# Inverse roots of the second layer's head norms: from GpSimd's power to Newton steps on VectorE

## The reference, cut to what matters

```python
attn = jax.nn.softmax(A1, -1) - lam * jax.nn.softmax(A2, -1)
O = jnp.einsum('bhqk,bhkd->bhqd', attn, V)
rms = jnp.sqrt(jnp.mean(O * O, -1, keepdims=True) + EPS)      # EPS = 1e-05
O = O / rms * rms_scale * (1.0 - LAMBDA_INIT)                 # LAMBDA_INIT = 0.8
O = O.transpose(0, 2, 1, 3).reshape(B, N, H * 2 * dh)
return O @ W_o.T
```

## Time and profile before

| what | us |
|---|---|
| timed runs | 1345.17, 1341.36, 1341.60 |
| median | 1341.6 |
| profiled execution, first to last instruction (span) | 1322.9 |
| PE busy in the span | 974.1 (74%) |
| DVE busy | 844.9 (64%) |
| ACT busy | 582.7 (44%) |
| POOL busy | 437.1 (33%) |
| mean granted TensorE clock | 0.852 of full |

### The profile page before, as it was taken

The page is one execution under the profiler, slowest core; times in us unless marked ns, Lnnn a source line. Parts: engine busy times, 40 slices in busy tenths (PEclk is TensorE's granted clock), DMA queues, the critical chain, the costliest instruction groups (busy, mean ns, idle before and its releaser), DMA issues.

```text
span 1322.9 us, 17363 instructions
## 1 busy us (share of the span) xinstructions
PE 974.1 (74%) x5741; PEld 575.7 (44%) x5741; DVE 844.9 (64%) x1977; ACT 582.7 (44%) x1409; POOL 437.1 (33%) x624
## 2 busy tenths in 40 slices
PE   6361565984985996888788878887878787776693
PEld 3241232453453564333334534444455454455583
DVE  1588879769988432665676656566555677644764
ACT  4344252462442343254454444344455554455363
POOL 0201441723724123022443132426311328433242
PEclk9685686996987998797898898778799999899897
DMA  7300000001000001000000000003134304233183
GB/s 223 110 0 0 1 0 1 1 1 36 1 1 1 0 1 42 7 1 0 1 1 1 1 0 0 1 0 117 56 109 128 106 16 131 67 119 104 54 270 114
DMA packets 54313, 60.40 MB, mean 46 GB/s; under 512 B 6208, under 2 KB 40656, under 8 KB 54224
## 3 DMA queue, kind: packets, MB, share of 16 engines
q1 hardware_dynamic: 52176, 55.10, 13.5%
q0 software_dynamic: 2048, 4.20, 1.0%
HBM read 46.05 MB, written 13.24 MB: 45 GB/s over the span
## 4 chain that ended last, share of the span: by engine, by line
PE 49%; DVE 22%; ACT 11%; issue 9%; POOL 6%; DMA 1%; SPq 0%; DVEq 0%; POOLq 0%; ACTq 0%
PE banks L792 8%; PE banks L849 5%; PE banks L935 5%; PE banks L839 4%; DVE MX L1444 3%; PE banks L627 3%; PE banks L802 3%; POOL oms L1943 3%; PE banks L805 2%; PE banks L679 2%; PE banks L867 2%; PE banks L909 2%; ACT PT L1760 2%; ACT yh L1695 2%; PE banks L874 2%
## 5 line engine op out<-in xcount | busy, mean ns | idle before, releaser
L1444 DVE TENSOR_REDUCE MX<-banks 128x4 f32<-128x512 f32 (+2 forms) x192 | 199.4, 1043 | 95.4 <-PE banks L909 93.6
L1920 POOL TENSOR_SCALAR_AFFINE_SELECT PT<-PT 128x256 f32<-128x256 f32 x256 | 105.9, 427 | 410.3 <-ACT PT L1760 410.1
L1760 ACT ACTIVATE PT<-banks 128x768 f32<-128x768 f32 (+1 forms) x192 | 168.0, 878 | 108.9 <-PE banks L867 108.1
L792 PE MATMUL banks<-xgT,wg 128*128 128x128 f32 x616 | 85.3, 282 | 39.2 <-ACT ysb L1721 35.7
L935 PE MATMUL banks<-PT,VA 128*17 128x512 f32 (+3 forms) x1024 | 101.5, 496 | 16.8 <-DVE on L1467 16.6
L874 PE MATMUL banks<-KS,QS 32*128 32x512 f32 (+3 forms) x512 | 97.8, 426 | 19.7 <-DVE MX L1444 15.2
L839 PE MATMUL banks<-w,hid 128*128 128x128 f32 x512 | 78.2, 301 | 45.5 <-DVE hid L1389 43.2
L839 PEld LDWEIGHTS banks<-w,hid 128*128 128x128 f32 x512 | 70.8, 209 | 79.9 <-DVE hid L1389 61.1
L867 PE MATMUL banks<-QS,KS 32*128 32x128 f32 (+3 forms) x512 | 94.0, 412 | 14.1 <-ACT PT L1760 9.0
L792 PEld LDWEIGHTS banks<-xgT,wg 128*128 128x128 f32 x616 | 74.4, 191 | 52.8 <-issue 50.4
L867 PEld LDWEIGHTS banks<-QS,KS 32*128 32x128 f32 x512 | 45.0, 196 | 95.4 <-issue 52.3
(11 more groups left out here) (273 smaller groups left out, 2055.2 us busy)
## 6 DMA issues: line engine op xcount, KB each, us to landing
wg<-in_ffn_dram SPq DMA_DIRECT2D x77, 386.0 KB, 3.3
yb<-ysb SPq DMA_DIRECT2D x17, 256.0 KB, 3.7
xg<-xs SPq DMA_DIRECT2D x16, 256.0 KB, 3.1
w<-in_ffn_w_dram SPq DMA_DIRECT2D x12, 256.0 KB, 5.2
xs<-zt SPq DMA_DIRECT2D x2, 1472.0 KB, 14.4
xs<-zt SPq DMA_DIRECT2D x1, 1984.0 KB, 13.3
x<-in_L_attn_x_dram SPq DMA_DIRECT2D x4, 256.0 KB, 5.0
out_dram<-x SPq DMA_DIRECT2D x16, 64.0 KB
```

What stands on the lines that cost most here:

```text
L792: mm = e.matmul(ps[:, at:at + cols], w, h, start=True, stop=True)
L1444: v_mx.at(e.tensor_reduce(MX[n % 2][:, u:u + nm, qb % 2, 2 * pair:2 * pair + 2, 24].rearrange("p s i -> p i s"), p4, AX.X, ALU.max, negate ...
L1760: a_p.at(e.activation(PT[q % 3][:, 2 * pair:2 * pair + 2, :], where["score", q, pair][:, :, 0:n], ACT.Exp, scale=ISQ8))
L1920: ins = e.affine_select(out=pt, in_=pt, compare_op=ALU.is_ge, fill=0.0, base=0, pattern=[[0, 2], [1, 128]], channel_multiplier=-1)
```

## The change

Step 3 goes away. DVE's `rms` takes over the inverse root itself: it halves the mean (times 1/32 plus 0.5e-5), makes a first guess of the root by integer-like arithmetic on the bits of the float (times -0.5 plus a constant, read and written as int32), and does three Newton steps of three instructions each, y <- y * (y*y*o - 1.5). Each instruction waits for the one before it. The three sign changes leave a negative root, for which the learned scale `rsc` gets the opposite sign. The roots are in a new tile `root`. `rms_o` waits for DVE's own semaphore. In the table `rms_o` moves from t + 6.5 to t + 4.0.

```diff
-        table += [(t, ("rms", n, part)), (t + 3.5, ("rms_p", n, part)), (t + 6.5, ("rms_o", n, part))]
+        table += [(t, ("rms", n, part)), (t + 4.0, ("rms_o", n, part))]
...
-        pw64 = sb("pw64", [128, 64])
...
+        root, step_ = sb("root", [128, 64]), sb("step", [128, 64])
...
-                v_own.at(e.tensor_scalar(rsc[:, :], rs0[:, :], 1.0 - 0.8, None, ALU.mult))
+                v_own.at(e.tensor_scalar(rsc[:, :], rs0[:, :], 0.8 - 1.0, None, ALU.mult))
...
             def rms(b, part):
-                o = means[:, :, heads[part]]
+                o, y, t = (tile[:, :, heads[part]] for tile in (means, roots, steps))
                 v.wait_ge(g_sq, 3 * b + part + 1)
                 n = v_own.at(e.tensor_reduce(o, osq[:, :, heads[part], :], AX.X, ALU.add))
                 v.wait_ge(v_own, n)
-                v_ms.at(e.tensor_scalar(o, o, 1.0 / 16.0, 1e-5, ALU.mult, ALU.add))
+                n = v_own.at(e.tensor_scalar(o, o, 1.0 / 32.0, 0.5e-5, ALU.mult, ALU.add))
+                v.wait_ge(v_own, n)
+                n = v_own.at(e.tensor_scalar(y.bitcast(mybir.dt.int32), o.bitcast(mybir.dt.int32), -0.5, 1593268703.0,
+                                             ALU.mult, ALU.add))
+                for i in range(3):
+                    v.wait_ge(v_own, n)
+                    n = v_own.at(e.tensor_tensor(t, y, y, ALU.mult))
+                    v.wait_ge(v_own, n)
+                    n = v_own.at(e.tensor_tensor(t, t, o, ALU.mult))
+                    v.wait_ge(v_own, n)
+                    n = v_own.at(e.scalar_tensor_tensor(out=y, in0=t, scalar=-1.5, in1=y, op0=ALU.add, op1=ALU.mult))
+                pr["root", b, part] = n
 
             def rms_o(b, part):
-                v.wait_ge(g_rs, 3 * b + part + 1)
+                v.wait_ge(v_own, pr["root", b, part])
...
-            def rms_p(b, part):
-                h0, h1 = PARTS[part]
-                o = oms[:, :].rearrange("p (q h) -> p q h", q=4)[:, :, h0:h1]
-                g_.wait_ge(v_ms, 3 * b + part + 1)
-                g_rs.at(e.tensor_tensor(o, o, pw64[:, 0:4 * (h1 - h0)].rearrange("p (q h) -> p q h", q=4), ALU.pow))
-
...
-            e.memset(pw64[:, :], -0.5)
```

More of the change, by code:

```diff
@@ L492, in build @@
             signal(n) for n in ("p_s", "a_p", "g_sel", "p_pv", "a_ov", "p_ot1", "v_on", "g_om"))
-        g_sq, v_ms, g_rs, v_o, p_to, a_to, p_wo1, v_xq, g_x1 = (
-            signal(n) for n in ("g_sq", "v_ms", "g_rs", "v_o", "p_to", "a_to", "p_wo1", "v_xq", "g_x1"))
+        g_sq, v_o, p_to, a_to, p_wo1, v_xq, g_x1 = (
+            signal(n) for n in ("g_sq", "v_o", "p_to", "a_to", "p_wo1", "v_xq", "g_x1"))
         p_tb, a_tb, v_out, v_xm, v_po, v_oh = (Signal(old.sem, 4) for old in (p_wo, a_oT, v_xt, v_dk, v_gm, v_vb))
@@ L1472, in _ @@
             width = [h1 - h0 for h0, h1 in PARTS]
-            means = oms[:, :].rearrange("p (q h) -> p q h", q=4)
+            means, roots, steps = (tile[:, :].rearrange("p (q h) -> p q h", q=4) for tile in (oms, root, step_))
             def rms(b, part):
-                o = means[:, :, heads[part]]
+                o, y, t = (tile[:, :, heads[part]] for tile in (means, roots, steps))
                 v.wait_ge(g_sq, 3 * b + part + 1)
@@ L1479, in rms @@
                 v.wait_ge(v_own, n)
-                v_ms.at(e.tensor_scalar(o, o, 1.0 / 16.0, 1e-5, ALU.mult, ALU.add))
+                n = v_own.at(e.tensor_scalar(o, o, 1.0 / 32.0, 0.5e-5, ALU.mult, ALU.add))
[10 more added lines that the diff above has]
+                pr["root", b, part] = n
             def rms_o(b, part):
-                v.wait_ge(g_rs, 3 * b + part + 1)
+                v.wait_ge(v_own, pr["root", b, part])
                 sq = osq[:, :, heads[part], :]
-                n = v_own.at(e.tensor_tensor(sq, om[b % 2][:, :, heads[part], :], means[:, :, heads[part]].unsqueeze(3)
+                n = v_own.at(e.tensor_tensor(sq, om[b % 2][:, :, heads[part], :], roots[:, :, heads[part]].unsqueeze(3)
                                              .broadcast_to([128, 4, width[part], 16]), ALU.mult))
@@ L1960, in _ @@
                         o_pw=o_pw, o_dk=o_dk, o_ol=o_ol, down=down, spread=spread, collect=collect,
-                        moe_x=moe_x, score=score, o_norm=o_norm, rms=rms,
-                        rms_p=rms_p, w_o=w_o)
+                        moe_x=moe_x, score=score, o_norm=o_norm, rms=rms, w_o=w_o)
             for job in order(table0, LATE0["POOL"]):
```

## The result

| | us (median, lowest to highest) | to before [95%] |
|---|---|---|
| before, measured beside it | 1343.38 (1341.36 to 1348.49) | |
| changed | 1362.38 (1358.03 to 1365.08) | 1.0136 [1.0102, 1.0171] |

The changed kernel is 19 us slower; +6.0 was forecast and the range ended at 1353. The sign was right, the size was three times too small. The profiled execution took 1358.03 us for a span of 1356.3 at a mean granted clock of 0.839.

The account below looks back on a forecast made before the run. The prediction saw no full engine but a web of short waits. Site gains and losses summed to +6.5 us, collisions and unseen slack to -0.5, so 1341.6 + 6.0 = 1347.6 us, with a range of 1335 to 1353.

Parts of the forecast that it names:

- the site walk: At each of the twelve normalization sites, PE's work shifted by the changed waits; gains and losses sum to +6.5 us.
- 1.0: Site with 32 columns: `rms_o` makes the second top 2.8 us later; a loss of 1.2 us was taken.
- 2.0: Site with 32 columns: 2.3 us of idle won against a 2.2 us block, second top late; loss 0.6 us.
- The stretch from 640 to 860 us: Six sites, 0.0 to 1.2, forecast to grow by +5.1 us together; no growth would prove the prediction wrong.
- Collisions with selects: Newton instructions on DVE beside POOL's selects: up to 0.2 us more each, adding 0 to 4 us in all.
- POOL's relief: The 45 us of powers taken off POOL; claimed to count nothing by itself.
- 17.1 us of idle against 25.2 of work: On DVE: idle before line 1485 that the power causes, traded for the Newton block's work at twelve sites.
- The chain's 33 us: Power's share of the chain from 600 us on, at eight of twelve sites; the prediction told readers to mistrust it.
- Rival (a): Chain view right: 33 us less 17 us of block, so -16, 1325.6 us; chance 0.16 in full or part.
- (b): Only DVE's balance counts and the new order is free: +3.4, 1345.0 us; chance 0.29 together with (c).
- (c): The web of waits absorbs both signs: 1341.6 us, plus or minus 2; chance 0.29 together with (b).
- (d): Newton meets selects at most sites, block 2.7 us instead of 2.1: 5.4 us added, 1353.0 us; chance 0.09.

Follow-up runs that it names:

- e4: Changed kernel without its three Newton steps, the root only guessed from the bits: 1315.49 us, 0.9775 of before.
- e8: Changed kernel with the three Newton steps at three places in DVE's list and `rms_o` back at t + 6.5: 1335.13 us, 0.9928 of before.
- e13: Changed kernel with sixteen spare PE matmuls before each of four waits for `v_o`: 1346.78 us, 1.0126 of before.
- e5: Changed kernel with POOL's twelve powers put back on a tile that nobody reads: 1353.86 us, 1.0072 of before.
- e15: The same kernel as e5, run again on another chip: 1338.64 us, 1.0076 of before.
- e12: Kernel before, power kept, with ten DVE instructions behind each `rms` whose results nobody reads: 1358.32 us, 1.0149 of before.
- e10: Changed kernel with two Newton steps, one in `rms` and one before `rms_o` at t + 6.5: 1331.73 us, 0.9915 of before.
- e3: Kernel before with POOL's power kept and only `rms_o` moved to its new place, t + 4.0: 1356.43 us, 1.0074 of before.
- e9: Changed kernel, no further edit, timed and profiled again: 1362.89 us, 1.0174 of before.

## Why the prediction was right in sign and wrong in size

**The step that failed** is the sum of the site walk, +6.5 us. It moved every PE instruction by the delay of what it waits for, and gave it the duration it had in the trace of before. That holds for the waits: of the 15.4, 20.3 and 13.0 us by which the stretch grew against the second profile of before, 6.3, 5.1 and 2.7 are waits. The other 9.1, 15.2 and 10.3 are matmuls that take longer, and the granted clock is lower there (0.87, 0.86 and 0.86 against 0.88). The walk had put this term at nothing. The prediction had the means for it: the earlier trace rows show a granted clock of 0.67 at 1.0, and it used 1.12 against 0.66 us for the four transposes there, to place an end, but never asked what the new waits would do to the clock. e4, e8 and e13 carry this: fewer waits, or none at one place, and the same matmuls are shorter at once. That a long wait lowers the clock is shown by filling one (e13 at 0.2). That the new waits at 2.0, 2.2 and 3.0 did is read from the order of events; no run fills those.

**Site by site.** Line 867's and the later matmuls' shifts give, from the first profile of before to the changed one, about -3.6 at 0.0, +1.0 at 0.1, +1.9 at 0.2, +2.6 at 1.0, +3.4 at 1.1, +2.5 at 1.2, +3.0 at 2.0, 0 at 2.1, +3.0 at 2.2, +2.9 at 3.0, -1.2 at 3.1 and 0 at 3.2: +15.5 in sum. Two of these hang on the first profile: with nothing changed, the second profile of before is itself 1.2 us longer over site 1.2 and 1.4 us over site 2.2. Against that one the change costs +1.4 and +1.6 there, as forecast. Eleven of twelve signs are as forecast (2.1's zero too); 3.2 is at 0 instead of +0.35, and 0.0 is better than -2.0. The misses in size that hold against both profiles are 1.0 (I took the value between low and full clock; a wait of 3.90 us is there), 1.1, 2.0 and 3.0, twice to eight times too small. The stretch from 640 to 860 us, forecast at +5.1, grew by about 9 to 10.5 us in the three profiles of the changed kernel. At 2.0, 2.2 and 3.0 the experts' matmuls then run at 2.02 to 2.05 us for eight instead of 1.13.

**The block.** Right: 0.17 to 0.19 us an instruction, steps spaced 0.20 to 0.23, no charge for int32, DVE +21.9 us. Collisions with selects are real and small (0.32 to 0.44 us instead of 0.18 to 0.19). Also right: POOL's relief is worth nothing (e5, e15).

**What hides the block.** The prediction set 17.1 us of idle against 25.2 of work as if they lay at the same place. e12 shows they don't: 13 us of the idle were filled and the kernel lost 11 to 29 us; the block comes ahead of the first top and the idle after it. e8 and e10 put more of the work behind the first top and turn the sign.

**The power's price** seems to have been more than 17.1 us too: e4 is 30 us faster. The chain's 33 us, which the prediction told the reader to mistrust, is nearer to that, perhaps by luck, since e4's 30 us aren't the power alone. Rival (a) fell not by that term but by the other: it took the block at 17 us, and its three steps cost 49. Rivals (b), (c) and (d) are all below the result; (d) has the wrong reason as well, each of its collisions adds 0.13 to 0.25 us.

**The base.** The trace of before was of a short execution (span 1322.9, 1333.0 in the next). The first pair of single profiles differs by 33 us, the medians by 19; 13 of the 33 are the piece near the end. The second profile's execution was 12 us below its own median as well, so the growths against it are likelier too large than too small.

**Still open:** how the 19 us split exactly between waits and clock (the profiles of one kernel differ by several us), what series of waits it takes to lower the clock, how much the new order adds to the block, and whether the dead power helps.

## What to carry to other kernels

Where PE's clock follows its waits, a delay ahead of an operation that opens PE's next work can cost more than its length (here 7 us of DVE cost 11 to 19, while e3's 10.4 us of idle cost about 10), and one removed can bring more: count the sum of waits, then ask for each longer wait at which clock the matmuls behind it run. Before a chain of small dependent instructions goes into a busy engine's list, cut it into pieces between the operations that others wait for; the same three steps made this kernel 0.9% slower as a block (1.2 to 1.7% with the early `rms_o`) and 0.7% faster in pieces. And take two profiles of the kernel before, when its times spread by 1%.

## What the hardware showed beyond that

- The clock made small things large: behind waits of 1.88 us for a late top and 0.49 for `hid` at 2.0 the granted clock went from 1.00 to 0.51, and the experts' eight matmuls from 1.13 to 2.05 us. Before the change a wait of 1.99 us at this site left it at 1.00.
- In a stretch with the same matmuls (3421 to 3425 records) PE was busy for 461 us at a granted clock of 0.91 (e4) and for 491 at 0.86 (e9).
- POOL's power takes 1.64, 4.17 and 5.47 us for 8, 24 and 32 columns, and run beside the changed kernel twelve times, waited for by nobody, it cost nothing. A multiply of 128x512 on DVE took 680 ns in the middle of one, as without it (681).
